# Stage 9 of a twelve-stage perceiver kernel: keys fetched one quarter ahead of their use instead of six, the second query selection moved to the front, small work moved between engines

## The reference

```python
def _L3_xattn_ref(hidden_states, context, attention_mask, q_w, q_b, k_w, k_b, v_w, v_b):
    q = _split_heads(hidden_states @ q_w.T + q_b)      # 16 heads of 16
    k = _split_heads(context @ k_w.T + k_b)
    v = _split_heads(context @ v_w.T + v_b)
    scores = jnp.einsum('bhqd,bhkd->bhqk', q, k) / jnp.sqrt(jnp.float32(HD))
    mask = (attention_mask > 0)[:, None, None, :]
    scores = jnp.where(mask, -jnp.inf, scores)
    probs = jax.nn.softmax(scores, axis=-1)
    ctx = jnp.einsum('bhqk,bhkd->bhqd', probs, v)
    ...
x = x + _L3_xattn_ref(_layernorm(x, axis=-1), ctx_1024, mask_BxS2_ik0, ...)
```

## Time and profile before

| | us |
|---|---|
| three runs | 1463.27, 1467.9, 1468.68 (median 1467.9) |
| the profiled execution | 1463.04 |
| its span, first to last instruction | 1460.9 |
| TensorE busy | 1386.2 (95%) |
| VectorE busy | 981.6 (67%) |
| ScalarE busy | 797.0 (55%) |
| GpSimd busy | 362.6 (25%) |

### The profile page before, as it was taken

One profiled execution on the slowest core, in us unless ns is written; L12 is line 12 of the kernel. 1 busy time (PEld: TensorE's weight loads), 2 busy tenths in 40 slices (PEclk: granted clock), 3 DMA queues, 4 the chain that ended last, 5 costly groups with the idle time before them and its releaser, 6 DMA issues.

```text
span 1460.9 us, 24247 instructions
## 1 busy us (share of the span) xinstructions
PE 1386.2 (95%) x9599; PEld 986.7 (68%) x9609; DVE 981.6 (67%) x1627; ACT 797.0 (55%) x1453; POOL 362.6 (25%) x461
## 2 busy tenths in 40 slices
PE   7799989999999999999999989999999998999997
PEld 5788657887898676898566654555555554645797
DVE  5776655334787576787367567989999983566433
ACT  5575335343665364664455426878888885315232
POOL 3685263001633113542101222222121100100000
PEclk9999999999999999999999999999999999999999
DMA  9313215334222433211317174444545304210140
GB/s 373 142 58 130 106 42 179 105 110 176 80 73 109 169 119 123 96 59 57 145 71 263 61 239 165 141 160 131 182 138 174 111 2 187 86 59 1 59 173 15
DMA packets 49071, 177.76 MB, mean 122 GB/s; under 512 B 4864, under 2 KB 6144, under 8 KB 43008
## 3 DMA queue, kind: packets, MB, share of 16 engines
q1 hardware_dynamic: 48960, 176.23, 33.7%
HBM read 132.66 MB, written 44.60 MB: 121 GB/s over the span
## 4 chain that ended last, share of the span: by engine, by line
PE 72%; DVE 15%; ACT 4%; POOL 3%; DMA 3%; issue 2%; SPq 0%; ACTq 0%; POOLq 0%; DVEq 0%
PE PS L160 50%; DVE SM L2397 8%; PE PS L2382 5%; PE PS L2286 4%; PE PS L630 2%; PE PS L2300 2%; DMA CT<-k_tiles 2%; PE PS L1874 1%; PE PS L1895 1%; POOL CNr L1342 1%; PE PS L2961 1%; PE PS L1902 1%; PE PS L2866 1%; DMA k_tiles<-CN 1%; DVE ARr L2414 1%
## 5 line engine op out<-in xcount | busy, mean ns | idle before, releaser
L2397 DVE TENSOR_REDUCE SM<-PS 128x1 f32<-128x1024 f32 x256 | 306.8, 1222 | 31.9 <-PE PS L2286 29.5
L160 PE MATMUL PS<-ARr 128*128 128x256 f32 (+1 forms) x1024 | 271.2, 336 | 0.6 <-POOL CNr L928 0.5
L160 PE MATMUL PS<-CNr,ARr 128*128 128x256 f32 (+1 forms) x952 | 202.1, 320 | 11.7 <-DVE ARr L797 11.4
L160 PEld LDWEIGHTS PS<-ARr 128*128 128x128 f32 x1024 | 181.1, 190 | 18.9 <-issue 0.7
L160 PEld LDWEIGHTS PS<-CNr,ARr 128*128 128x128 f32 x952 | 154.1, 194 | 26.6 <-DVE ARr L797 13.1
L160 PE MATMUL PS<-ARr,HTr 128*128 128x512 f32 x384 | 121.7, 398 | 0.5 <-ACT CN L459 0.5
L2286 PE MATMUL PS<-ARr 64*128 64x512 f32 x320 | 117.1, 448 | 5.1 <-ACT AR L2469 2.8
L858 ACT CAST ARr<-PS 128x512 fp32r<-128x512 f32 x96 | 56.3, 586 | 113.4 <-PE PS L630 113.4
L2300 PE MATMUL PS<-ARr 64*128 64x256 f32 x640 | 116.5, 304 | 1.3 <-DVE ARr L2414 1.0
L2469 ACT ACTIVATE AR<-PS 128x512 f32<-128x512 f32 x172 | 93.5, 605 | 23.4 <-PE PS L2300 14.0
L2469 ACT ACTIVATE CT<-PS 128x512 f32<-128x512 f32 x168 | 91.2, 602 | 18.6 <-PE PS L2300 15.3
(11 more groups left out here) (412 smaller groups left out, 2799.0 us busy)
## 6 DMA issues: line engine op xcount, KB each, us to landing
CT<-k_tiles SPq DMA_DIRECT2D x64, 512.0 KB, 5.0
CN<-ctx_n SPq DMA_DIRECT2D x24, 1024.0 KB, 5.7
k_tiles<-CNr SPq DMA_DIRECT2D x32, 768.0 KB, 3.5
CT<-pack SPq DMA_DIRECT2D x6, 2048.0 KB, 7.6
CT<-ctx_t SPq DMA_DIRECT2D x8, 1024.0 KB, 19.5
k_tiles<-CN SPq DMA_DIRECT2D x32, 256.0 KB, 4.1
AR<-pack SPq DMA_DIRECT2D x16, 512.0 KB, 3.5
v_ones<-CN SPq DMA_DIRECT2D x28, 288.0 KB, 3.2
```

The lines of the kernel that those rows point to most:

```text
L160: last = te.matmul(o, l, r, start=first and k == 0, stop=final and k == n - 1, skip_group_check=True)
L2397: ve.tensor_reduce(MX9[:, p % 2, e, g % 2, g % 8 // 2:g % 8 // 2 + 1], PS[:, b:b + 2, :].rearrange("p a b -> p (a b)"), AX, ALU.max).then_inc(
```

## The change

It has six parts.

1. Keys: in step n quarter n//2 + 6 is fetched and cast instead of n//2 + 11; in the start three quarters beyond the first four instead of eight. Step n+2 is the one that needs quarter n//2 + 6.
2. Jobs: six instead of ten in the start ("kvkvvv"), nine instead of five in the loop, keys in steps 1, 9, 17, 25, 33 and values in steps 5, 13, 21, 29.
3. The second selection follows the first, in banks 0 to 3, and VectorE brings it out.
4. The turned rows are added by one instruction over all partitions instead of two copies of one partition each.
5. The addition of a pair's result to x moves from VectorE to GpSimd, with two buffers `t9`.
6. `weights_pool_1` moves to the front of `pool_1`.

```diff
-                             ("t9", "k"), ("s9", "kvvkvvvvvv"), ("heads", "k" * 5)):
+                             ("t9", "k"), ("s9", "kvkvvv"), ("heads", "kvkvkvkvk")):
...
         def pool_1(pl):
             ge = pl.e
+            weights_pool_1(pl)
             pl.wait_ge(*w1)
...
-            weights_pool_1(pl)
             jobs_pool(pl, "t1b")
...
         for p in range(5):
             PAIR_JOBS[8 * p + 1] = jobs.pop(0)
+            if jobs:
+                PAIR_JOBS[8 * p + 5] = jobs.pop(0)
...
                 if u == 0:
                     yield "select", 0, 0
+                    yield "select", 1, 0
                     yield ("job", *jobs.pop(0))
                 yield "best", u // 2, u % 2
-                if u == 8:
-                    yield "select", 1, 0
...
-                for e in range(2):
-                    r = slice(64 * e + 32, 64 * e + 33)
-                    ve.tensor_copy(QQ9[r, pr, cols], bank("rows", p)[r, 0:256]).then_inc(*dv.inc("turn", "mrow", 9, p))
+                rows = QQ9[:, pr, cols]
+                ve.tensor_tensor(rows, bank("rows", p)[:, 0:256], rows.bitcast(F32), ALU.add).then_inc(
+                    *dv.inc("turn", "mrow", 9, p))
...
+                if what == "select" and n == 1:
+                    for pr in range(4, 8):
+                        dv.wait_ge(("sel_ps", 1))
+                        ve.tensor_scalar(QQ9[:, pr, :], bank("sel", pr), W9["ones2"], None, ALU.add).then_inc(
+                            *dv.inc("proj", "qm", pr))
...
-                if n < 8:
+                if n < 3:
                     keys_pool(pl, 4 + n)
             for what, n, k in pair_steps():
-                if what in ("beside", "both") and n % 2 == 0 and n and k == 0 and n // 2 + 11 < 64:
-                    keys_pool(pl, n // 2 + 11)
+                if what in ("beside", "both") and n % 2 == 0 and n and k == 0 and n // 2 + 6 < 64:
+                    keys_pool(pl, n // 2 + 6)
                 if what == "job":
                     job_pool(pl, n, k)
+                if what == "finish":
+                    b2, pr, _ = of_pair(n)
+                    x = X[:, 2 * b2:2 * b2 + 2, 32 * pr:32 * pr + 32]
+                    pl.wait_ge(("fin_out", 9, n), ("fin", 9, n - 1) if n else ("row", 9, 3))
+                    pl.e.tensor_tensor(x, x, t9[n % 2].rearrange("p i e r -> p i (e r)"), ALU.add).then_inc(
+                        *pl.inc("mixed", "fin", 9, n))
...
-                if what in ("beside", "both") and n % 2 == 0 and n and k == 0 and n // 2 + 11 < 64:
-                    fetch(sp, n // 2 + 11)
+                if what in ("beside", "both") and n % 2 == 0 and n and k == 0 and n // 2 + 6 < 64:
+                    fetch(sp, n // 2 + 6)
```

More of the change, by code:

```diff
@@ L2189, in perceiver @@
         MX9, ri9 = sm(2, 2, 2, 4), sm(2, 2, 2)
-        t9 = sm(2, 2, 16)
+        t9 = [sm(2, 2, 16) for _ in range(2)]
         QQ9 = view(ARr, 0, 8, 512)
@@ L2267, in perceiver @@
         BP9, SR9 = banks.ring((0, 1), (2, 3)), banks.ring((4,), (5,), (6,))
-        PB4, FJ9 = banks.ring((4,), (5,), (6,), (7,)), banks.ring((2,))
+        PB4, PA4 = banks.ring((4,), (5,), (6,), (7,)), banks.ring((0,), (1,), (2,), (3,))
         K9 = banks.ring((3,))
@@ L2327, in select @@
             def select(n):
-                got = [PB4.take(("sel", 4 * n + k), ("qm", 4 * n + k)) for k in range(4)]
+                got = [(PA4 if n else PB4).take(("sel", 4 * n + k), ("qm", 4 * n + k)) for k in range(4)]
                 pe.wait_ge(*[p for _, before in got for p in before], ("q_rest", n))
@@ L2346, in pe_9 @@
                 if what == "job":
-                    job_pe(pe, FJ9 if (n, k) == JOBS["s9"][0] else SR9, n, k)
+                    job_pe(pe, SR9, n, k)
                 if what == "select":
@@ L2438, in dve_9 @@
                     ps = bank("fin", n)[:, 0:68].rearrange("p (i e r) -> p i e r", i=2, e=2)
-                    x = X[:, 2 * b2:2 * b2 + 2, 32 * pr:32 * pr + 32]
                     dv.wait_ge(("fin_ps", 9, n), ("fin_out", 9, n - 1) if n else None)
                     ve.reciprocal(ri9[:, n % 2], ps[:, :, :, 16]).then_inc(*dv.inc("mixed", "ri", 9, n))
-                    dv.wait_ge(("ri", 9, n), ("fin", 9, n - 1) if n else ("row", 9, 3))
-                    ve.tensor_tensor(t9, ps[:, :, :, 0:16], ri9[:, n % 2].unsqueeze(3).to_broadcast([128, 2, 2, 16]),
+                    dv.wait_ge(("ri", 9, n), ("fin", 9, n - 2) if n > 1 else None)
+                    ve.tensor_tensor(t9[n % 2], ps[:, :, :, 0:16], ri9[:, n % 2].unsqueeze(3).to_broadcast([128, 2, 2, 16]),
                                      ALU.mult).then_inc(*dv.inc("mixed", "fin_out", 9, n))
-                    dv.wait_ge(("fin_out", 9, n))
-                    ve.tensor_tensor(x, x, t9.rearrange("p i e r -> p i (e r)"), ALU.add).then_inc(
-                        *dv.inc("mixed", "fin", 9, n))
                     if n == 15:
@@ L2476, in act_9 @@
                 if what == "select":
-                    for pr in range(4 * n, 4 * n + 4):
+                    for pr in range(4 * n, 4 * n + 4) if n == 0 else ():
                         ac.wait_ge(("sel_ps", n))
```

## The result

The changed kernel takes 1492.6 us (median of 4 runs, 1488.0 to 1494.1), the one before 1465.6 (4 runs, 1463.3 to 1468.7): ratio 1.0178, 95% interval 1.0143 to 1.0212, some 26 us slower. The forecast was 1493. The profiled execution took 1491.2 us, its span 1489.3.

The account below looks back on a forecast made before the run. TensorE, busy 95% of the span, was taken as the bound, so changes pay only where it waits. Terms -5.0 - 9.6 + 19 + 14 + 5.7 + 7 - 3 + 0.2 = +28 gave 1493 us, range 1469 to 1505.

Parts of the forecast that it names:

- the main step: Pairs 0 to 4: key quarters fetched behind a key job's store come late, and TensorE waits 3.8 us each time.
- weights of stage 2: End of stage 1: moved GpSimd weight work removes TensorE's idle time and half clock; 5.0 us gained, bounds 3 to 6.
- start, to the first key job of pair 1: Stage 9's start: pairs begin 6.8 us earlier, ScalarE's store waits go; 9.6 us gained up to that job.
- late keys, five waits: Pairs 0 to 4: quarter ready 12.95 us after job start, needed at 9.18; five waits of 3.8, 19 us.
- clock behind them: Behind each key wait: half speed for 5.6 us, 2.8 us lost each, 14 us for five; bounds 0 and 3.9 each.
- four value jobs in the pairs: Steps 5, 13, 21, 29: 1.91 us of TensorE each, not hidden; one counted in the start, three more 5.7 us.
- steps 57 to 64: Second half of values: fetch stands behind SyncE's wait for products; four fetches late, 7 us lost, bounds 2 and 9.
- VectorE's small work: Pairs: one turn copy and one add less, 0.2 us by 15 pairs, 3 us gained; bounds 0 and 9.
- Rival 1: Key waits three steps after a key job: quarters arrive in time, -12 us, 1451 to 1456; chance 0.09.
- Rival 2: Pairs 0 to 4: keys late but the clock holds, +14 us, 1477 to 1482; chance 0.22.
- the clause at the end of that paragraph: Start of stage 9: values in AR are stored ahead of the pairs, so both ScalarE waits go.
- the worst case that I took from it, 5.1: Stage 2's weights: each of four VectorE normalisations waits for a 1.27-us GpSimd subtraction, 5.1 us in all; gain then 2.7.

Follow-up runs that it names:

- by order: Changed kernel with each key quarter's fetch issued one step earlier on SyncE, in front of the key job's store: 1450.5 us, ratio 0.9906.
- by lead: Changed kernel with six quarters fetched in the start instead of three and quarter n/2+9 at step n instead of n/2+6: 1451.1 us, ratio 0.9907.
- the short lead alone: Kernel before with three quarters fetched in the start instead of eight and quarter n/2+6 at step n instead of n/2+11: 1488.4 us, ratio 1.0151.
- the key edit alone: Kernel before with three quarters fetched in the start, then quarter n/2+7 at odd step n, in front of the job's store: 1455.0 us, ratio 0.9933.
- the run with the old job table: Changed kernel with the fetch one step earlier, ten jobs in the start, five key jobs and no value job in the pairs: 1441.9 us, ratio 0.9853.
- the run with the filled waits: Changed kernel with 14 matmuls of 128x512 bf16 in front of each of the five late maxima: 1477.6 us, ratio 1.0086.

## Why the prediction was right, step by step

The time, the sign and the main step held: each priced part, tried by itself, and what it measured (ratio differences times 1465 us, each good to some 3 to 6 us):

| term | forecast | measured |
|---|---|---|
| weights of stage 2 | -5.0 | -6.3 |
| start, to the first key job of pair 1 | -9.6 (-11.5 without the value job in it) | -9.8 (a run without that job) |
| late keys, five waits | +19 | +18.8 |
| clock behind them | +14 | +9 (traces), +13.5 (times) |
| four value jobs in the pairs | +5.7, and 1.9 within the start's term | +7.8 |
| steps 57 to 64 | +7 | +8.5 |
| VectorE's small work | -3 | -2.8 (trace), -5 (times) |
| sum | +28 | +23 to +30; the kernel: +26 |

*Late keys.* The chain from job to cast was 12.78 us for 12.95. That two repairs of it, by order and by lead, give the same 40 us back (waits, clock and steps 57 to 64 together: 36 to 41 by the table), and that the short lead alone brings five waits into the kernel before, shows it. Rival 1 (in time) needed the chain under 9.2 us; it falls by the trace. (A step takes one maximum per head, not two as the prediction has it; its sums use the right number.)

*Clock.* Rival 2 (the clock holds) falls: all five waits had 0.50 behind them, and filling them brought time back. The Trainium skill (TensorE: Matmul & The Clock Gate, HAM oscillation) has every round of such a loop pay, and the trace agrees: five of five, for 3 to 5 us. My 2.8 us for each was too much by the traces, which have 1.8, and right by the times, which have 2.7.

*Steps 57 to 64* came near (7 for 8.5), but not as I had it. I priced four late fetches and no clock, and my own numbers (6.5 us against 5.0 to 5.5) give 1 to 1.5 us each, not up to 2.5. There were two waits, 4.3 us in all, and half clock for 3.5 and 5.7 us behind them, which loses an estimated 4.5 us (half of the two stretches). That the sums agree is luck.

*The start* came out in size, but the cause that I gave is not the one that the runs show. My sum from the first selection to the start of the pairs was 34.9 us; the changed kernel has 35.9 (829.34 to 865.26). I put the 6.8 us gained down to the second selection's place and to six jobs instead of ten. The queries gave nothing (0.9850 without, 0.9853 with), and ten jobs took as long as six (39.24 and 39.13 us). In the kernel before, with its ten jobs, the key edit alone brings all 9.8 us: it is the clause at the end of that paragraph, the stores of values that no longer stand behind key fetches. With six jobs the stores behind fetches hold nothing up either: with six fetches in the start, one behind each job, it took 39.31 us. So fewer fetches are enough by themselves; fewer jobs may be too, but no run has them without the other edits. I had added up the length of the start rightly and put the gain down to two edits that it did not need; in that the term was lucky.

Two things can explain why ten jobs took no longer than six; no run separates them. With six jobs TensorE had fallen to half clock by the end of the start. The stretch from 858 to 863 in the changed kernel, 28.7 us behind its first selection:
```profile
858.00:863.00 5.00, 4.82 (x11) 2.29 (x10) 4.75 (x7) 0.00 (x0) 0.86 (x1) 0.50 0.98 302
```
And 28.4 us behind the first selection (at 825.34) with ten jobs, in the run with the old job table:
```profile
853.70:858.00 4.30, 4.30 (x20) 2.74 (x19) 3.43 (x5) 0.38 (x1) 1.71 (x2) 1.00 0.36 141
```
And without a job TensorE waits for a reduction in front of each two maxima of the start, as in this row of the changed kernel's timeline:
```profile
854.80 0.73 PE L2287 MATMUL PS<-CTr,ARr 64*128 64x512 f32 x2 [0.40 <-DVE SM L2398]
```
A value job there fills such waits; in the pairs, where TensorE is full, it costs its length.

*Weights.* The gain was right (6.3 us by the times; by the traces 5.3, since the first product of `HTr` in stage 2 starts at 219.22 instead of 224.54), its price not: beside GpSimd's last casts, subtractions and an addition the four normalisations took 3.97 us, 2.6 more than alone, not 0.8. Here the row that I chose (other GpSimd work beside the same instructions) misled, and the rule of the Trainium skill (SBUF — State Buffer, Who interferes with whom) was the better guide, though the worst case that I took from it, 5.1, was not reached. The section has the rule for VectorE's two-port modes, which it says instructions of this kind can enter. No run shows that the ports are the cause here. The cover hid it either way.

*The version that beats both* is the short lead with the fetch in front of the store, the old job table, and the change's weights and small edits: 1441.9 with the queries' new order, 1442.6 without it, 1.5% below the kernel before.

## What to carry to other kernels

On a queue that issues in program order, price a shorter lead by the whole chain that stands ahead of the fetch, from the engine that feeds the store in front of it; and look first whether the fetch can be issued ahead of that store. Fewer prefetches can also be a gain, where stores of other data queue behind their buffer waits (as with ten jobs in the start; with six, three more fetches cost nothing). Before moving filler work, see in which stretch the bounding engine really has room: the same job was free in a stretch that VectorE bounds and cost its full length in one where TensorE is full.

## What was not expected of the hardware

How long TensorE had waited did not by itself decide whether the clock fell. In the kernel before it stayed at 1.00 behind 2.85 us of idle time; in the run with the filled waits it fell behind 1.84 us, and in the changed kernel behind 1.68. TensorE's timeline of the filled run:
```profile
1056.48 0.46 PE L2287 MATMUL PS<-ARr 64*128 64x512 f32 x1 [1.84 <-issue]
```
And the stretches before and behind it:
```profile
1052.00:1056.50 4.50, 2.66 (x32) 1.49 (x31) 3.07 (x5) 2.17 (x4) 1.16 (x2) 1.00 0.92 295
1056.50:1060.00 3.50, 3.50 (x28) 1.84 (x28) 1.81 (x2) 2.08 (x4) 0.16 (x1) 0.59 0.79 258
```
What decides it stays open.
